# A two-layer macaron transformer on one core: the output projection of attention in f32 instead of split f16

## The reference

```
ctx = softmax(scores) @ v            # per head, then heads side by side: 512 x 256
x   = x + ctx @ Wo.T                 # layer 0
x   = x + ctx @ Wo + bo              # layer 1
```

## Time and profile before

| what | us |
|---|---|
| median of 3 runs | 565.31 (565.25 to 566.36) |
| profiled execution, first to last instruction (span) | 563.3 |
| outside the span (median less span) | 2.0 |
| PE busy | 536.7 |
| DVE, ACT, POOL busy | 455.5, 400.5, 343.1 |

### The profile page before, as it was taken

The page is one execution under the profiler, slowest core; times in us unless marked ns, Lnnn a source line. Parts: engine busy times, 40 slices in busy tenths (PEclk is TensorE's granted clock), DMA queues, the critical chain, the costliest instruction groups (busy, mean ns, idle before and its releaser), DMA issues.

```text
span 563.3 us, 12960 instructions
## 1 busy us (share of the span) xinstructions
PE 536.7 (95%) x5060; PEld 303.1 (54%) x5060; DVE 455.5 (81%) x813; ACT 400.5 (71%) x605; POOL 343.1 (61%) x427
## 2 busy tenths in 40 slices
PE   8998888999999999999899999999999999999997
PEld 7564644545554654556446564465455645654664
DVE  4799899997989698599986879878898768794453
ACT  5996675786587778765785848867778587688533
POOL 2467999855987588744456374634563735444634
PEclk9999999999999999999999999999999999999999
DMA  8800110301040102122010120010102011201201
GB/s 322 340 2 0 51 64 2 113 22 60 2 144 12 42 1 78 55 72 71 2 41 10 43 71 21 3 61 8 66 21 61 1 41 73 60 21 42 78 37 38
DMA packets 20525, 31.76 MB, mean 56 GB/s; under 512 B 7360, under 2 KB 8768, under 8 KB 20312
## 3 DMA queue, kind: packets, MB, share of 16 engines
q1 hardware_dynamic: 20464, 30.94, 15.8%
HBM read 13.75 MB, written 2.36 MB: 29 GB/s over the span
## 4 chain that ended last, share of the span: by engine, by line
PE 59%; DVE 15%; POOL 7%; ACT 6%; issue 5%; DMA 3%; SPq 3%; DVEq 0%; POOLq 0%; ACTq 0%
PE PS L593 16%; PE PS L704 11%; PE PS L617 9%; DVE MX L1058 5%; PE PS L669 5%; PE PS L684 4%; PE PS L635 4%; ACT PB L846 3%; PE PS L719 3%; PE PS L577 3%; DMA X<-x_in 2%; PE PS L541 2%; PE PS L651 2%; DVE ST L871 1%; DVE MX L1054 1%
## 5 line engine op out<-in xcount | busy, mean ns | idle before, releaser
L846 ACT ACTIVATE PB<-PS 128x1024 f32<-128x1024 f32 x160 | 157.2, 1024 | 50.0 <-PE PS L684 41.7
L1058 DVE TENSOR_REDUCE MX<-PS 128x2 f16<-128x1024 f32 (+2 forms) x192 | 157.7, 866 | 20.2 <-PE PS L541 19.5
L593 PE MATMUL PS<-XT,WGU 128*128 128x512 f16 x660 | 156.3, 380 | 1.7 <-ACT PB L846 0.5
L1134 POOL TENSOR_TENSOR HH<-TH,HH 128x512 f16<-128x512 f32 x71 | 82.6, 1177 | 70.4 <-ACT HH L814 70.4
L1162 POOL TENSOR_SCALAR_AFFINE_SELECT PB<-PB 128x512 f32<-128x512 f32 (+1 forms) x140 | 74.5, 560 | 69.7 <-ACT PB L846 69.7
L593 PEld LDWEIGHTS PS<-XT,WGU 128*128 128x128 f16 x660 | 59.1, 98 | 73.8 <-issue 6.2
L617 PE MATMUL PS<-WD,HH 128*128 128x256 f16 x660 | 77.3, 273 | 0.1
L704 PE MATMUL PS<-PB,V 128*32 128x512 f32 (+3 forms) x1024 | 75.5, 435 | 1.4 <-POOL PB L1162 1.1
L617 PEld LDWEIGHTS PS<-WD,HH 128*128 128x128 f16 x660 | 62.8, 98 | 11.7 <-issue 2.0
L814 ACT ACTIVATE HH<-TH 128x512 f16<-128x512 f32 (+1 forms) x86 | 52.2, 627 | 20.0 <-DVE TH L1004 7.1
L669 PE MATMUL PS<-SK,SQ 63*128 63x256 f16 (+3 forms) x512 | 58.8, 299 | 5.9 <-DVE MX L1054 2.2
(11 more groups left out here) (117 smaller groups left out, 783.7 us busy)
## 6 DMA issues: line engine op xcount, KB each, us to landing
SQ<-QPB SPq DMA_DIRECT2D x24, 256.0 KB, 2.5
OC<-OT SPq DMA_DIRECT2D x16, 256.0 KB, 2.4
RB<-scratch SPq DMA_DIRECT2D x64, 64.0 KB, 2.2
SK<-QPB SPq DMA_DIRECT2D x12, 256.0 KB, 2.5
SQ<-MT SPq DMA_DIRECT2D x128, 1.0 KB
out<-X SPq DMA_DIRECT2D x8, 256.0 KB, 2.1
PB<-gu SPq DMA_DIRECT2D x2, 704.0 KB, 6.3
LATE<-gu SPq DMA_DIRECT2D x2, 704.0 KB, 14.6
```

The costliest lines, as they stand in the source:

```text
L593: m = e.matmul(o[:, :], WGU[l][:, k, col:col + P], rows_of(f)[j][:, k, :], start=j == 0 and k == 0, stop=j == 1 and k == 1)
L846: e.activation(PB[Q % 2][:, j, :, :], two_banks("s", i), ACT.Exp, scale=0.25).then_inc(a_exp, 1)
L1058: e.tensor_reduce(mx[:, :, pr, t], o[:, :, col:col + (t + 1) * P], AX.X, ALU.max, negate=True).then_inc(a_max, 1)
L1134: e.tensor_tensor(hh[1][:, s * T:(s + 1) * T], value_of(j)[0], hh[0][:, s * T:(s + 1) * T], ALU.subtract).then_inc(f_lo, 1)
```

## The change

The normalised context and the output weights stay in f32. `CH` becomes one f32 tile and `WO` one f32 tile a layer. POOL step `c` writes its product straight to `CH`. ACT step `c` and POOL step `C` are gone (16 letters of each), and four ACT steps and two POOL steps that prepared the output weights (four and two `w` letters); the letters that remain stand in the same order, and the orders of PE, DVE and SP are unchanged. `WO` is loaded by DMA directly, without the factor WS, and the projection is two products a tile in place of six. The waits are renumbered; POOL step `c` takes over the wait for the projection of the attention before (`t_om`).

```diff
-        WO = [sb(f"WO{l}", [P, 2, 2, D], F16) for l in range(2)]
+        WO = [sb(f"WO{l}", [P, 2, D]) for l in range(2)]
...
-        CH = [sb(f"CH{j}", [P, 2, T], F16) for j in range(2)]
+        CH = sb("CH", [P, 2, T])
...
-            e.dma_start(ro[0], wo0).then_inc(l_a0, 16)
+            e.dma_start(WO[0][:, :, :], wo0).then_inc(l_a0, 16)
...
-                    w.wait_ge(t_lo, 2 * (n - 1) + u + 1)
+                    w.wait_ge(t_cc, 2 * (n - 1) + u + 1)
...
-                    w.wait_ge(p_act, 7 if l == 0 else 11)
-                    w.wait_ge(p_pool, 5 if l == 0 else 7)
-                    for s, (jc, jw, g) in enumerate((jc, jw, g) for jc, jw in TERMS for g in range(2)):
-                        w.wait_ge((t_hi, t_lo)[jc], 2 * n + g + 1)
-                        m = e.matmul(o[:, q * D:(q + 1) * D], CH[jc][:, g, t * P:(t + 1) * P], WO[l][:, jw, g, :],
-                                     start=s == 0, stop=s == 5)
+                    wait_projections(w, l)
+                    for g in range(2):
+                        w.wait_ge(t_cc, 2 * n + g + 1)
+                        m = e.matmul(o[:, q * D:(q + 1) * D], CH[:, g, t * P:(t + 1) * P], WO[l][:, g, :],
+                                     start=g == 0, stop=g == 1)
...
-                        l, s = divmod(i - 3, 4)
+                        l, s = divmod(i - 3, 2)
...
-                elif c == "c":
-                    n, u = divmod(i, 2)
-                    w.wait_ge(t_cc, i + 1)
-                    w.wait_ge(t_om, 4 * n)
-                    w.wait_ge(p_dve, 14)
-                    e.activation(CH[0][:, u, :], OC[:, u, :], ACT.Copy).then_inc(t_hi, 1)
...
-                    e.scalar_tensor_tensor(xv, bank("o", i), 1.0 / (CS * WS), xv, ALU.mult,
+                    e.scalar_tensor_tensor(xv, bank("o", i), 1.0 / CS, xv, ALU.mult,
...
-                    e.tensor_tensor(OC[:, u, :], OC[:, u, :], RB[:, u, :], ALU.mult).then_inc(t_cc, 1)
-                elif c == "C":
-                    n, u = divmod(i, 2)
-                    w.wait_ge(t_hi, i + 1)
-                    e.tensor_tensor(CH[1][:, u, :], OC[:, u, :], CH[0][:, u, :], ALU.subtract).then_inc(t_lo, 1)
+                    w.wait_ge(t_om, 4 * n)
+                    e.tensor_tensor(CH[:, u, :], OC[:, u, :], RB[:, u, :], ALU.mult).then_inc(t_cc, 1)
```

More of the change, by code:

```diff
@@ L127 @@
     "act":
[L128 to L133, removed]
+        "TwwXxxwttthwhtXthhxxtkktthhwXtwhhkkkttYtyyxxhhhXhtttQhvQwvkktYtyyQtQxhhhxhhtTQQkteeeeQtQeeehhoeeetee"
+        "heeotehYoeeeteehhoeeevveeyyeoeeQeeQXoxxeeeQtQttheethhoteeeehteYoeehhvvyyeeeeXoxxeeeeQQttthXhheettheo"
+        "teexhxQhoeeeeetQhotthttvYhvyyhhthQeQeeQeeeeeeeoXexxeeotetehhtthteXthhheeoxxeeettohYvttyyeeehhQtetQeh"
+        "hQeheoeeeXxxeeoetteeethhheoteeXhtthhoeeveeeeeoexexYttteyyhQQQheehttethehhoeeeeeeoeeeXoexxveXttthhhtt"
+        "theheheexxeYeooyytehQQeeeQtteeeeoetXohhhvtteeeeehhxxoeeteeehttXhheoeeteeteeeeeoxxhthohtthhtthththhXx"
+        "xthtthththhth",
     "pool":
-        "wwwrrhrhhhhwdwdherhhhshasqaddqessaaqqhhhssaahhqqwwssaaffqfdqfdfhffhefffhffhfffhccCCssaaqfffrqssdaaqq"
-        "fffhdheffcfhfhhCdcdffrCssaafrfqqhfshahfffhhsfcffaqqheCcChhhhfffddrffffrffhhhhhbfffechhcCChhbhdfdffrf"
-        "ffrhfffhhhhccCCeffffhhhhhffbddfffrrhhhhhccCCffeffrffbfffhhhhhccCCfrffhhffffffhhhcChchChhhrhhhhh",
+        "wwwrrhrhhhhwddherhhhshasqaddqessaaqqhhhssaahhqqwssaaffqfdqfdfhffhefffhffhfffhccssaaqfffrqssdaaqqfffh"
+        "dheffcfhfhhdcdffrssaafrfqqhfshahfffhhsfcffaqqhechhhhfffddrffffrffhhhhhbfffechhchhbhdfdffrfffrhfffhhh"
+        "hcceffffhhhhhffbddfffrrhhhhhccffeffrffbfffhhhhhccfrffhhffffffhhhchchhhhrhhhhh",
     "banks":
@@ L268, in macaron_kernel @@
         t_dc, t_oc, t_so, t_si = ([sem(f"t_{n}{u}") for u in range(2)] for n in ("dc", "oc", "so", "si"))
-        t_rc, t_cc, t_hi, t_lo, t_bo, t_om, t_res = (sem(n) for n in ("t_rc", "t_cc", "t_hi", "t_lo", "t_bo", "t_om", "t_res"))
+        t_rc, t_cc, t_bo, t_om, t_res = (sem(n) for n in ("t_rc", "t_cc", "t_bo", "t_om", "t_res"))
         o_out = sem("o_out")
@@ L275, in macaron_kernel @@
         rd = [OC[:, :, :].rearrange("p u t -> p (u t)").rearrange("p (c n) -> p c n", c=4),
-              CH[0][:, :, :].rearrange("p u t -> p (u t)").bitcast(F32).rearrange("p (c n) -> p c n", c=2)]
+              CH[:, 0, :].rearrange("p (c n) -> p c n", c=2)]
         late = [LATE[:, k, :] for k in range(2)]
@@ L286, in macaron_kernel @@
               raw[0][:, 4 * HID + FC * D:].rearrange("p (k n) -> p k n", k=2)]
-        ro = [RB[:, l, :].rearrange("p (c n) -> p c n", c=2) for l in range(2)]
         spare = PB[1][:, :, :, :].rearrange("p s a n -> p (s a n)")
@@ L338, in wait_exp @@
                 if j == NS_T - 1:
-                    w.wait_ge(p_act, 9)
-                    w.wait_ge(p_pool, 6)
+                    w.wait_ge(p_act, 7)
+                    w.wait_ge(p_pool, 5)
         def wait_x(w, b, l, was, pair=None):
@@ L389, in wait_lo, with wait_projections @@
                 w.wait_ge(f_lo, (FC - 1) * f + ci)
+        def wait_projections(w, l):
+            if l == 0:
+                w.wait_ge(l_a0, 48)
+            else:
+                w.wait_ge(l_a1, 32)
         def wait_bank(w, c, i):
@@ L459, in sync_program @@
             e.dma_start(ra[1], wqkv1).then_inc(l_a1, 16)
-            e.dma_start(ro[1], wo1).then_inc(l_a1, 16)
+            e.dma_start(WO[1][:, :, :], wo1).then_inc(l_a1, 16)
             for c in order:
@@ L515, in sync_program @@
                     w.wait_ge(t_cc, 2 * (n - 1) + u + 1)
-                    w.wait_ge(p_act, 11)
-                    w.wait_ge(p_pool, 7)
                     src = scratch[n % 2, u].rearrange("(a g s) t -> a g (s t)", a=4, g=2)
@@ L629, in tensor_program @@
                     o = bank("q", i)
-                    w.wait_ge(p_act, 7 if l == 0 else 11)
-                    w.wait_ge(p_pool, 5 if l == 0 else 7)
+                    w.wait_ge(p_act, 5 if l == 0 else 7)
+                    w.wait_ge(p_pool, 4 if l == 0 else 5)
                     for s, (jw, jx) in enumerate(TERMS):
@@ L741, in scalar_program @@
                             w.wait_ge(l_a1, 32)
-                        src, dst = (ra[l], WA[l]) if s < 2 else (ro[l], WO[l])
-                        if s % 2 == 0:
-                            e.activation(src, src, ACT.Copy, scale=WS).then_inc(p_act, 1)
+                        if s == 0:
+                            e.activation(ra[l], ra[l], ACT.Copy, scale=WS).then_inc(p_act, 1)
                         else:
                             w.wait_ge(p_act, i)
-                            e.activation(dst[:, 0, :, :], src, ACT.Copy).then_inc(p_act, 1)
+                            e.activation(WA[l][:, 0, :, :], ra[l], ACT.Copy).then_inc(p_act, 1)
                 elif c == "k":
@@ L1093, in pool_program @@
                     else:
[L1095 to L1098, removed]
+                        l = i - 3
+                        w.wait_ge(p_act, 3 + 2 * l + 2)
+                        e.tensor_tensor(WA[l][:, 1, :, :], ra[l], WA[l][:, 0, :, :], ALU.subtract).then_inc(p_pool, 1)
                 elif c == "r":
```

## The result

The changed kernel takes 571.99 us (4 runs, 571.6 to 572.8) against 565.4 us: a ratio of 1.0112 (95% interval 1.0090 to 1.0133), 6.6 us slower. In a later comparison it took 572.18 us against 564.39, a ratio of 1.0135 (1.0119 to 1.0150). The forecast was 569.3 us, slower than before.

The account below looks back on a forecast made before the run. From 100 us on, PE's queue was taken to bound the kernel. Terms 4.9 - 0.4 - 0.5 = +4.0 us gave a 567.3 us span, plus 2.0 us between span and median: 569.3 us, range 565.0 to 573.0.

Parts of the forecast that it names:

- PE's term: Projection L719: two f32 products a tile for six f16 ones, +0.21 us a tile, +6.7 us of PE work over 32 tiles.
- I let the growth go through in the same share: 6.7 x 0.73 = +4.9 us: Projection L719: 16.9 of its 23.2 us lie on the chain, so 73% of the added PE work reaches the end.
- PE pays all of it: Rival, chance 0.14: PE, busy 97% from 100 to 540 us, pays all growth and more, 572.0 to 573.5 us.
- The sign that I gave for a wrong pass-through: PE's idle time shrinking by as much as L719 grew would show the 73% share reaching the end to be wrong.
- the other sign: The forecast falls if L846 waits leave PE's list altogether or new waits for DVE stand behind the projections.
- The relief: ACT loses 16 roundings, POOL 16 subtractions; PE's shorter waits give back 0.4 and 0.5 us.
- The 0.4 us for the last low part: Last attention's projection: PE's weight loads at L719 no longer wait for POOL's low part, -0.4 us.
- The 0.5 us: ACT's freed time lets exponentials, and through them PE, go earlier: -0.5 us, nearest bound 4.4 us.
- PE's waits are not at these places: Reason for the small estimate for ACT's freed time: PE does not wait where roundings and subtractions are removed.
- the third rival: Chance 0.10: the rounding blocks ACT's queue with exponentials behind it; ACT's freed time decides, faster, 563.1 us.
- Costs set at nothing: Dropped weight-preparation copies, weight DMAs, DVE step o's constant, SP's waits and the moved projection wait: each 0.
- their covers: Weight preparation: waits for DVE or POOL absorb the dropped copies; without them, up to 2.4 us on either engine.

Follow-up runs that it names:

- the relief alone: Kernel before with six f16 products kept, ACT's 16 roundings and POOL's 16 subtractions removed, low part of the context zero: 564.71 us against 564.86, ratio 0.9991.

## Why the prediction was right, and where it was not

**The size of PE's term was right.** Two matmuls for an f32 product, two clock ticks a column, 216 ns a step, 128 matmuls, 3.45 us for 16 without a run's edges: all as worked out from L704 and L577. Missing was the first step behind narrow products, 320 ns where it was 120: it grows by 0.200 us, the sum counts 0.107 for a step, and 5 x 0.093 makes 0.5 us. The term is 6.7 + 0.5 = 7.2 us; the runs grew by 6.85 us, and the last of them would have grown by 0.30 more without the wait that it lost.

**The step that failed is "I let the growth go through in the same share: 6.7 x 0.73 = +4.9 us".** All of it went through. The alignment shows it run by run, PE's idle time from 100 to 540 us did not shrink (12.6 us, where it was 11.8 and a fall was forecast), and eight f16 products (+7.2 us for 7.0) show it without f32. The share of a line on the chain says where that line stood in the chain of one execution; it is no measure of what growth of the line passes. A run of projections that was off the chain still pushed all that stands behind it in PE's order. That PE had no slack at these places is read from the alignment. The rival "PE pays all of it" (0.14), 572.0 us, is what happened, though its number fits better than its parts: 7.2 us of growth, 0.5 us of relief, 1.4 us lost at 217 and 242 to 248 us and a few tenths absorbed. I had the row for it: PE busy 97% from 100 us on. The sign that I gave for a wrong pass-through, idle time that shrinks by as much as L719 grew, was the wrong way round: that would have been absorption. Of the other sign, new waits for DVE behind the projections, there is one, L983's 0.66 us, and not right behind a projection.

**The relief came out smaller in the net: 0.9 us taken, 0.15 measured** on the kernel before (0.9991, an interval that doesn't exclude 0.9), and 0.5 us on the changed one (572.71 to 572.18). The 0.4 us for the last low part was real as a mechanism (0.30 us in the trace). The 0.5 us was put on ACT's exponentials, and those waits hardly moved. But "PE's waits are not at these places" was wrong: at 380 us a rounding held up ACT's copy of a bank and through it PE's transposes, 0.2 us in the kernel before and 0.7 to 0.9 us once PE's work had grown. This is the mechanism of the third rival, on another instruction and far too small to decide; 0.55 us at 217 us and the 0.89 at 242 to 248 us outweighed it. That the freed time of ACT and POOL would turn into idle time held in the main: ACT -9.2 and POOL -20.4 us of busy time.

**Costs set at nothing held.** From 70 us to the first projection the matmuls of the changed kernel start within 0.05 us of their time before (0.84 us earlier in a second profile of it, which has no dip of the clock), and the first profile shows no gain from the dropped copies of the output weights, as their covers said; as the two profiles differ by 0.9 us there, this stays open. The wait for the projection before at POOL's product is nowhere in the list of waits.

**The range held the result, the forecast's middle did not.** The low end came from absorption, of which there was none upwards. The errors, -1.8 for the pass-through, -0.5 for the first steps and -0.75 for the relief, come to -3.1 us, against the -2.7 between 569.3 and 571.99; the 0.4 is within what two comparisons of the same pair differ by (6.6 and 7.8). That the sum closes is in part luck, since the relief's net hides losses and gains of 0.5 to 0.9 us that nobody forecast.

## What to carry to other kernels

When PE is busy 97% of a stretch in a hand-made order, as here, cost growth on PE at its full size, whatever the chain's share of that line; cost a saving at half of it or less until the waits behind it are read, for here +7 us cost 7.2 and -7 us gave 3.6. An f32 product of 256 columns takes as much of PE (2 x 216 ns) as four f16 ones (4 x 109 ns), so two for six is eight for six. The copies that it spares are worth what PE waits for them, not what they take on engines that idle anyway; count also the waits for what stands behind a copy in its engine's queue, for they grow when PE's work shifts.

## What the runs showed of the hardware that was not expected

The 0.55 us at 217 us, which came and went between kernels, is a contest of DVE and POOL. DVE's L1009 subtracts two tiles of SBUF, POOL's L1162 cuts a triangle in SBUF, and both become ready at nearly the same time. In the kernel before:

```profile
216.42 0.64 POOL L1162 TENSOR_SCALAR_AFFINE_SELECT PB<-PB 128x512 f32<-128x512 f32 x1
216.43 1.17 DVE L1009 TENSOR_TENSOR HH<-TH,HH 64x512 f16<-64x512 f32 x1
```

and with the relief alone (L1004 and L1158 there):

```profile
216.45 0.68 DVE L1004 TENSOR_TENSOR HH<-TH,HH 64x512 f16<-64x512 f32 x1
216.45 1.18 POOL L1158 TENSOR_SCALAR_AFFINE_SELECT PB<-PB 128x512 f32<-128x512 f32 x1
...
217.77 1.07 PE L704 MATMUL PS<-PB,V 128*32 128x512 f32 x8 [0.53 <-POOL PB L1158]
```

The one that wins takes its 0.64 or 0.68 us, and the other takes 1.17 or 1.18, nearly both together. Over the whole trace of the kernel before, the five of L1009 that start while a POOL instruction has 0.2 us or more to go last 758 to 1641 ns, the other ten 684 to 704. When POOL loses here, the probability product waits 0.53 us and all behind it is late; when DVE loses, nobody on PE minds. In all ten traces the two starts lie within 10 ns of each other. DVE loses in six, among them the kernel before; POOL loses in four, among them both profiles of the changed kernel. In the changed kernel's first profile POOL starts 4 ns ahead and loses all the same, so the last few nanoseconds can't be read from the starts. A change that touches neither instruction moved all that follows by 0.55 us, 0.1% of the time. The Trainium skill describes this on the page "SBUF — State Buffer", section "SBUF: two separate sides": a VectorE instruction with two SBUF inputs and a GpSimd instruction that reads SBUF arbitrate for a shared port pair, whoever starts first holds it as an exclusive lock for the whole instruction, and the other blocks. The traces agree in the main: in the kernel before POOL ends at 217.06 us and DVE, which takes 0.68 us alone, 0.54 us later.
